# Joining the attention and the second FFN in one block, and beginning the FFN within the attention's last two slots

## The reference, cut to what matters

```
x = x + 0.5 * ffn(layernorm(x))      # first FFN
x = x + attention(layernorm(x))      # causal, 16 heads of 32, rotary, tanh soft cap
x = x + 0.5 * ffn(layernorm(x))      # second FFN, the same weights

def ffn(h):
    z = w_norm * h / rms(h)
    p = softmax(z @ w_router); top 4 of 32 experts for each token, in expert order, 128 slots an expert
    routed = sum over chosen experts of p * (silu(z @ w_gate) * (z @ w_up)) @ w_down
    shared = sigmoid(z @ w_sgate) * (silu(z @ sw_gate) * (z @ sw_up)) @ sw_down
    return h + routed + shared
```

## Time and profile before

| | |
|---|---|
| median of 3 runs | 1000.01 us |
| profiled execution | 997.65 us |
| its span, first to last instruction | 995.9 us |
| TensorE busy | 921.9 us, 93% |
| VectorE busy | 691.1 us, 69% |
| ScalarE busy | 534.3 us, 54% |
| GpSimd busy | 502.7 us, 50% |
| TensorE's mean granted clock | 0.983 |

### The profile page before, as it was taken

One profiled execution on the slowest core, in us unless ns is written; L12 is line 12 of the kernel. 1 busy time (PEld: TensorE's weight loads), 2 busy tenths in 40 slices (PEclk: granted clock), 3 DMA queues, 4 the chain that ended last, 5 costly groups with the idle time before them and its releaser, 6 DMA issues. The chain is left out here.

```text
span 995.9 us, 18354 instructions
## 1 busy us (share of the span) xinstructions
PE 921.9 (93%) x6274; PEld 690.3 (69%) x6274; DVE 691.1 (69%) x1702; ACT 534.3 (54%) x798; POOL 502.7 (50%) x534
## 2 busy tenths in 40 slices
PE   1999998999999899999999999839999989999997
PEld 1778885777778765666666666427888857777786
DVE  4888768644444769989989999646887676453435
ACT  3667652223233478878878878726666522232322
POOL 5342112565553467877878877623422124565630
PEclk9999999999999999999999999978999999999999
DMA  5432316677774510010010000112323156777735
GB/s 192 121 93 91 102 53 180 160 180 183 173 186 82 169 65 23 21 42 21 21 42 21 21 22 12 62 35 90 113 89 95 60 172 157 180 180 183 187 44 169
DMA packets 95434, 101.91 MB, mean 102 GB/s; under 512 B 18689, under 2 KB 86657, under 8 KB 95361
## 3 DMA queue, kind: packets, MB, share of 16 engines
q1 hardware_dynamic: 83072, 83.17, 27.3%
q0 software_dynamic: 12288, 17.83, 10.6%
HBM read 65.44 MB, written 35.54 MB: 101 GB/s over the span
## 5 line engine op out<-in xcount | busy, mean ns | idle before, releaser
L86 PE MATMUL gu<-x_hi,gu_hi 128*128 128x512 f32 x264 | 122.9, 465 | 4.0 <-DVE act_gu L1145 3.8
L691 POOL DMA_INDIRECT rows<-z_rows,slots x64 | 68.5, 1071 | 76.0 <-DVE slots L1136 57.3
L977 ACT CAST a_hi<-act_gu 128x512 fp32r<-128x512 f32 x96 | 59.2, 616 | 86.9 <-DVE act_gu L1145 74.5
L1570 ACT ACTIVATE capped_at<-scores_at 128x2048 f32<-128x2048 f32 x64 | 93.3, 1457 | 23.3 <-PE scores_at L1470 23.0
L87 PE MATMUL gu<-x_hi,gu_lo 128*128 128x512 f32 x264 | 105.6, 400 | 0.0
L88 PE MATMUL gu<-x_lo,gu_hi 128*128 128x512 f32 x264 | 105.6, 400 | 0.0
L1578 ACT ACTIVATE probs_at<-capped_at 128x2048 f32<-128x2048 f32 x64 | 95.2, 1487 | 2.5
L1639 POOL TENSOR_SCALAR_AFFINE_SELECT probs_at<-probs_at 128x1024 f32<-128x1024 f32 x64 | 86.6, 1357 | 18.4 <-ACT probs_at L1578 17.7
L86 PE MATMUL down<-down_hi,a_hi 128*128 128x256 f32 x300 | 94.2, 314 | 0.2 <-DVE a_lo L1155 0.2
L267 POOL TENSOR_TENSOR rstd_f<-var_in_f,neg_half 128x8 f32<-128x8 f32 x16 | 26.7, 1668 | 126.0 <-DVE var_in_f L262 126.0
L1025 ACT ACTIVATE y<-gu,rows 128x256 f32<-128x256 f32 x64 | 30.3, 473 | 109.9 <-PE gu L906 106.0
(11 more groups left out here) (245 smaller groups left out, 2605.5 us busy)
## 6 DMA issues: line engine op xcount, KB each, us to landing
w_gu<-in_w_gate SPq DMA_DIRECT2D x64, 176.0 KB, 2.6
w_gu<-in_w_up SPq DMA_DIRECT2D x64, 176.0 KB, 3.2
w_down<-in_w_down SPq DMA_DIRECT2D x64, 176.0 KB
z_rows<-z SPq DMA_DIRECT2D x16, 512.0 KB, 3.1
acc<-base SPq DMA_DIRECT2D x10, 512.0 KB, 3.4
out<-base SPq DMA_DIRECT2D x10, 512.0 KB, 3.4
x_f<-in_X SPq DMA_DIRECT2D x8, 512.0 KB, 4.6
xn_at<-acc SPq DMA_DIRECT2D x16, 256.0 KB, 2.7
```

The source lines that it names most:

```text
L86: nc.tensor.matmul(out, w_hi, x_hi, start=first, stop=False)
L691: pool.indirect_dma_start(out=gathered_rows[:, n, :], out_offset=None, in_=m.z_rows, in_offset=bass.IndirectOffsetOnAxis(ap=slots[:, e:e + ...
L1570: nc.scalar.activation(capped[:, u % 2, :, 0:n], scores[:, :, 0:n], ACT.Tanh, scale=QK_SCALE / SOFTCAP).then_inc(capped_ready, 1)
```

## The change

All three stages stand in one block, so the meeting of engines, the clearing of semaphores and the second meeting between attention and second FFN are gone; all semaphores are cleared once, at the end. Both FFNs use the same semaphores: `sem` hands out the existing one and notes what value the first FFN left it at, and every wait adds that value (`reached`). Some small tiles are placed earlier in memory so that what the FFN writes first doesn't lie on tiles the attention still uses.

The second FFN's first block is interleaved with the end of the attention:

- SyncE issues the loads of blocks 0 and 1 in slot 12 instead of slot 14.
- VectorE: `statistics` of block 0 opens slot 14, that of block 1 opens slot 15; the low parts of block 0 follow `divide(14, 1)` in slot 15.
- GpSimd: `scales` of block 0 stands ahead of slot 14's first `causal`, that of block 1 ahead of slot 15's first `causal`.
- ScalarE: two of the four `z` rows of block 0 after the second exponential of slot 14, two at that slot's end; the high parts in slot 15, ahead of its third cap.
- TensorE: `turn(0)` in slot 15, behind `weighted_values(14, 3)` and three waits; `output(14)` also waits for the low parts.
- The tail of sequence 15 is mixed into a new first slot of the second FFN, `slot_behind`, on all compute engines.

In the first FFN, the splitting of the attention's weights (11 pairs, L202 and L207) starts at piece 98 instead of 102.

The core of the diff (the shared semaphores' many lines are cut to a few; in all of the FFN's functions `wait_ge` becomes `reached`):

```diff
+        def sem(name, total=0):
+            if name not in m.shared:
+                m.shared[name] = (nc.alloc_semaphore(name=name), total)
+                ...
+            else:
+                begun[m.shared[name][0]] = m.shared[name][1]
+            return m.shared[name][0]
+
+        def reached(engine, signal, value):
+            engine.wait_ge(signal, begun.get(signal, 0) + value)
...
-        SPLITS_FROM = 3 * PIECES
+        SPLITS_FROM = LEAD + 5 * E // 2
...
@@ ffn, on_sync
             store_z(0)
             load_x(2)
             store_z(1)
+            if before:
+                before.wait_stored(sp)
...
@@ ffn, on_gpsimd
+            if before:
+                before.last_output(pool)
             make_base(0)
             for r in range(1, NB - 2):
-                front.scales(pool, r, r % 2)
+                if r > 1 or not before:
+                    front.scales(pool, r, r % 2)
                 make_base(r)
...
@@ ffn, on_tensor
+            def slot_behind(f, r, s):
+                before.scores_taken(pe)
+                chunk(0, 0)
+                before.residual_added(pe, SEQS - 1)
+                router(0)
+                before.tensor_last_values(pe)
+                turn_logits(f)
+                chunk(0, 1)
+                chunk(0, 2)
+                before.tensor_last_output(pe)
+                chunk(0, 3)
+                before.residual_added(pe, SEQS)
+                turn(r)
+                count(f)
+                chunk(0, 4)
+                router(r)
+                chunk(0, 5)
+                turn_logits(r)
+                for c in range(6, GU):
+                    chunk(0, c)
+                ...
...
@@ ffn, on_scalar
+            def slot_behind(f, r, s):
+                make_z(1)
+                before.probabilities_made(act)
+                silu_of(0, 0)
+                take_logits(0)
+                before.scalar_last_values(act)
+                silu_of(0, 1)
+                x_hi_parts(r)
+                exponentials(f)
+                a_hi_part(0, 0)
+                take_logits(r)
+                ...
...
@@ ffn, on_vector
+            def slot_behind(f, r, s):
+                before.vector_last_values(dve)
+                product(0, 0)
+                before.vector_last_low_part(dve)
+                top_experts(f)
+                before.vector_last_residual(dve)
+                x_lo_parts(r)
+                product(0, 1)
+                take_counts(f)
+                statistics(s)
+                before.sequences_stored(dve)
+                weigh(f)
+                a_lo_part(0, 0)
+                a_lo_part(0, 1)
+                product(0, 2)
+                top_experts(r)
+                ...
...
@@ attention, tensor_slot
             if behind:
                 weighted_values(b - 1, 1 - q, 3)
+            if following:
+                pe.wait_ge(v_copied, SEQS)
+                pe.wait_ge(turned_ready, SEQS * PIECES)
+                pe.wait_ge(x2_ready, SEQS - 2)
+                following.turn(0)
...
             score_unit(b, q, 3)
+            if following:
+                following.input_split(pe)
             if behind:
                 output(b - 1)
...
@@ attention, scalar_slot
             if further:
                 normalise(b + 2, held)
+            elif following and ahead:
+                following.make_z(0, range(0, 2))
+            elif following:
+                act.wait_ge(roped_ready, (SEQS - 1) * PIECES + 2)
+                following.x_hi_parts(0)
             cap(b, 2)
...
             if ahead:
                 copy_v(b + 1, 1 - q)
+                if following:
+                    following.make_z(0, range(2, TJ))
...
@@ attention, gpsimd_slot
             if further:
                 root(b + 2)
+            elif following:
+                following.front.scales(pool, b - (SEQS - 2), b - (SEQS - 2))
             causal(b, 0)
...
@@ attention, vector_slot
             if further:
                 statistics(b + 2)
+            elif following:
+                following.front.statistics(dve, b - (SEQS - 2), b - (SEQS - 2), 0)
...
+            if following and not ahead:
+                dve.wait_ge(roped_ready, (SEQS - 1) * PIECES + 2)
+                following.x_lo_parts(0)
...
+        def wait_stored(sp):
+            for n in range(HELD):
+                sp.wait_ge(stored[n], 16 * len(range(n, SEQS, HELD)))
+            sp.sem_inc(all_stored, 1)
...
+        def last_output(pool):
+            pool.wait_ge(out_ready, SEQS)
...
+        def tensor_last_values(pe):
+            weighted_values(SEQS - 1, 1, 3)
+            denominators(SEQS - 1, 1)
...
+        def scalar_last_values(act):
+            take_values(SEQS - 1, 1)
+            y_hi_part(SEQS - 1, 0)
+            y_hi_part(SEQS - 1, 1)
+
+        def vector_last_values(dve):
+            y_lo_part(SEQS - 1, 0)
+            invert(SEQS - 1, 1)
+            divide(SEQS - 1, 1)
...
@@ attention, on_sync
-                if b == SEQS - 2:
+                if b == SEQS - 4:
...
@@ build
-            run(ffn_before, middle)
-            run(ffn(nc, m, "2", m.acc2, front, ins))
-            nc.clear_and_free_semaphores(fronts.signals)
+            last = ffn(nc, m, "2", m.acc2, front, ins)
+            run(ffn_before, middle, last)
+            for stage in (fronts, ffn_before, middle, last):
+                nc.clear_and_free_semaphores(stage.signals)
             nc.all_engine_barrier()
```

More of the change, by code:

```diff
@@ L509, in ffn @@
[L509 to L520, removed]
+        z_ready = sem("z_ready", TJ * NB)
@@ new lines, in router, with make_z @@
+        def router(r):
+            reached(pe, lo_ready, KC * (r + 1))
+            h = held(r)
+            for k in range(KC):
+                last = split_matmul(nc, zT[0][:], m.router_hi[:, k, :], m.router_lo[:, k, :], x_hi[h][:, k, :],
+                                    x_lo[h][:, k, :], k == 0, k == KC - 1)
+            last.then_inc(lT_ready, 1)
+        def make_z(r, pieces=range(TJ)):
+            q = r % 2
+            reached(act, front.scales_ready, r + 1)
+            at_least(act, zT_ready, KC * (r - 1))
+            at_least(act, z_stored[q], 16 * (r // 2))
+            for j in pieces:
+                nc.scalar.activation(z[:, q, j, :], x[:, q, j, :], ACT.Identity, bias=front.z_shift[:, q, j:j + 1],
+                                     scale=front.z_scale[:, q, j:j + 1]).then_inc(z_ready, 1)
@@ L843, in slot @@
                     router(s)
+            def slot_behind(f, r, s):
[18 more added lines that the diff above has]
+                    chunk(0, c)
+                count(r)
+                turn(s)
+                for j in range(TJ):
+                    down_proj(0, j, range(MT))
+                router(s)
             def piece(p):
@@ L907, in down_expert @@
                 last.then_inc(y_ready, 1)
-            turn(0)
-            router(0)
-            for b in range(MERGED):
+            if before:
+                slot_behind(*ROUTES[0])
+            else:
+                turn(0)
+                router(0)
+                slot(0, *ROUTES[0])
+            for b in range(1, MERGED):
                 slot(b, *ROUTES[b])
@@ L1269, in copy_products @@
             def copy_products(e):
-                dve.wait_ge(prodT_ready, e + 1)
+                reached(dve, prodT_ready, e + 1)
                 at_least(dve, y_ready, e - 1)
                 dve.tensor_copy(prodT[:, e % 2], prodT_ps).then_inc(prodT_copied, 1)
-            statistics(1)
-            x_lo_parts(0)
-            if weights:
-                weights.low_gate_up(dve)
-            for b in range(MERGED):
+            if before:
+                slot_behind(*ROUTES[0])
+            else:
+                statistics(1)
+                x_lo_parts(0)
+                if weights:
+                    weights.low_gate_up(dve)
+                slot(0, *ROUTES[0])
+            for b in range(1, MERGED):
                 slot(b, *ROUTES[b])
@@ L1519, in output, with tensor_slot @@
             last.then_inc(out_ready, 1)
[L1521 removed]
+        def tensor_slot(b, q, behind=True, ahead=True, further=True, following=None):
             score_unit(b, q, 0)
@@ L1813, in on_tensor, with on_scalar @@
             tensor_slot(SEQS - 2, 0, further=False)
-            tensor_slot(SEQS - 1, 1, ahead=False, further=False)
-            weighted_values(SEQS - 1, 1, 3)
-            denominators(SEQS - 1, 1)
-            output(SEQS - 1)
-        def on_scalar(act, following=None):
+            tensor_slot(SEQS - 1, 1, ahead=False, further=False, following=following)
+        def on_scalar(act, before, following):
             scalar_slot(0, 0, 2, behind=False)
@@ L1845, in on_gpsimd, with on_vector @@
             gpsimd_slot(SEQS - 3, 1)
-            gpsimd_slot(SEQS - 2, 0, further=False)
-            gpsimd_slot(SEQS - 1, 1, ahead=False, further=False)
-            front.scales(pool, 0, 0)
-        def on_vector(dve, following=None):
```

(3 more changed lines are left out.)

448 lines of the change are left out of this document (247 added, 201 removed).

## The result

The changed kernel takes 990.7 us (median of 7 runs, 988.74 to 994.77) against 998.06 us of the kernel before beside it (995.9 to 1000.85): ratio 0.9926, 95% interval 0.9904 to 0.9949. Measured once more, beside the last experiments (e9), it is 989.87 us, 0.9903 [0.9882, 0.9924]. The forecast was 988.5 us, with 979.0 to 995.0 as its range, and faster.

The account below looks back on a forecast made before the run. TensorE bounds the kernel almost everywhere except the seam between attention and second FFN. Terms +3.1 + 4.3 + 1.0 - 0.5 - 19.6 - 0.7 = -12.4, plus 0.9, give -11.5: 1000.0 to 988.5 us, range 979.0 to 995.0.

Parts of the forecast that it names:

- slow restart: Down projection of block 0: TensorE restarts at a lower clock after idling between chunks 7 and 8, +0.9 us (0 to 3).
- The chain and its end: Seam: one chain followed up to weigh(0), set there by VectorE alone; what is gained there is gained at the end.
- Change 5: First FFN: earlier splits shorten TensorE's 1.48 us wait for block 7's product, -0.7 us (bounds 0 and -1.5).
- Change 3: Tail of sequence 15, last exponential to end of output(15): 13.3 us instead of 13.8, -0.5 us.
- Change 4: End of output(15) to weigh(0): 10.0 us instead of 29.6, set by block 2's load, -19.6 us.
- Change 1: Slots 14 and 15: GpSimd's scales ahead of the masks delay TensorE's weighted values, +3.1 and +4.3 us.
- Change 2: Slot 15: after TensorE's longer wait the score unit also runs at half clock, +1.0 us.
- The rival that the masks aren't delayed: Slots 14 and 15: exponentials pace the masks, so the 8.4 us loss is absent, 980.1 us; chance 20%.
- The rival of a persisting half clock: Half clock lasts from slot 15 into block 0, +6.1 us, 994.6 us; chance 15%.

Follow-up runs that it names:

- e9: The changed kernel as it is, timed again beside e10 and e11: 989.87 us, 0.9903 of the kernel before.
- e1: The changed kernel without the interleaving in slots 14 and 15, with the joining and earlier splits kept: 990.27 us, 0.9921 of the kernel before.
- e5: The changed kernel plus 16 and 36 unused filler matmuls in TensorE's waits for the masks of slots 14 and 15: 988.69 us, 0.9926 of the kernel before.
- e10: The kernel of e5 timed again, beside e9: 988.01 us, 0.988 of the kernel before.
- e7: e3 with statistics(0) between VectorE's two turns of sequence 15 and rotary work ahead of slot 14's scales on GpSimd: 979.66 us, 0.983 of the kernel before.
- e2: The changed kernel with GpSimd's scales of block 1 behind slot 15's second mask instead of ahead of its first: 985.13 us, 0.9865 of the kernel before.
- e3: e2 with slot 14's scales behind its first mask too, and all four z products at slot 14's end: 984.55 us, 0.9872 of the kernel before.
- e4: The changed kernel with VectorE's statistics of block 2 behind block 0's third product instead of ahead of weigh(0): 991.76 us, 0.9938 of the kernel before.
- e11: The kernel of e3 timed again, code unchanged: 985.14 us, 0.9849 of the kernel before.
- e6: The kernel before with only the first FFN's earlier splits: 997.11 us, 1.0004 of the kernel before.
- e8: e7 with statistics, z and turning of block 2 moved later in the second FFN's block 0: 980.34 us, 0.9833 of the kernel before.

## Why the prediction was right, point by point

The direction, the chain and the gain were right; the closeness of the number is in part luck. The change of the median is -7.4 us and that of the profiled executions -8.9, where -11.5 was forecast. The losses were forecast too small by 5.0 us (2.7 for masks and clock, 2.3 for the tail); 2.2 of these are hidden by the first FFN's part and by the slow restart that didn't come, which have other causes. And the forecast starts from a median of 1000.0 us, while the kernel before took 998.06 beside the changed one: that alone brings 988.5 nearer to 990.7 by 2 us.

**The chain and its end** held. From `weigh(0)` to the end of the kernel it is 307.4 us before and 307.3 after, so the sum up to `weigh(0)` is the result. Between slot 14's first scores and `weigh(0)` it is, in the prediction's own terms:

| term | forecast | measured |
|---|---|---|
| up to slot 14 (Change 5) | -0.7 | -2.0 |
| slot 14's first scores to the last exponential (Changes 1 and 2) | +8.4 | +11.1 |
| last exponential to the end of `output(15)` (Change 3) | 13.3 - 13.8 = -0.5 | 15.6 - 13.8 = +1.8 |
| end of `output(15)` to `weigh(0)` (Change 4) | 10.0 - 29.6 = -19.6 | 10.0 - 29.6 = -19.6 |
| slow restart in block 0 | +0.9 | 0 |
| sum | -11.5 | -8.7 (span: -8.9) |

The measured ones are differences of the rows above: (654.17 - 610.28) - (645.06 - 612.31), then 669.75 - 654.17 (GpSimd's base starts as `output(15)` ends), then 679.73 - 669.75.

**Change 4**, the gain, came as worked out: the load decides, and VectorE waits 2.45 us for it. e1 divides the 19.6 us. It joins the stages and changes no slot, and gets 8.2 of them (29.6 to 21.4 us): that is the meeting. The other 11.4 are first steps of the second FFN that stand ahead of `output(15)` now, and the interleaving pays for them with the 11.1 and 1.8 us of the table.

**Change 1** has the right mechanism and nearly the right size. With the clock filled up, e5 and e10 reach the last exponential 40.7 us after slot 14's first scores, against 32.75 before: +8.0, where 7.4 was forecast. In e7, with the masks ahead, it is 34.6. The 0.6 between them is no more than what GpSimd's rows add: in each of the two scales one small instruction took some 0.7 instead of 0.2 us. e2 and e3 show the cause: with the scales behind the masks, the waits shrink. The rival that the masks aren't delayed (20%) is out. Slot 14's weighted values came 3.6 us later (3.1 forecast), slot 15's 10.2 (7.4), and the latter includes the clock.

**Change 2**, the clock, is the step that was mis-sized: 1.0 us forecast, and 11.1 - 8.0 = 3.1 measured, or 2.8 by e9 and e10 (43.6 - 40.7). I took half clock for slot 15's score unit alone. It stood in slot 14 as well, behind a wait of 2.28 us, and in slot 15 it lasted through the score units and the first ten matmuls of `output(14)` (0.41 instead of 0.28 us each). The row for this was at hand: the earlier trace rows has 1.94 us behind a wait of 2.31, and slot 14's new wait was forecast at about that length. It was only asked of slot 15. How long it lasts isn't fixed: in e9, the same kernel, it ends within slot 15's score unit (1.72 us), and `output(14)` runs at full clock. The rival of a persisting half clock (15%) is right in kind, not in place: block 0 ran at full clock. The Trainium skill, "TensorE: Matmul & The Clock Gate", Part 1, says that half rate is the default and that activity releases it. The trace agrees: a clock of 0.57 follows the wait of 5.39 us, and in e5, with fillers in the waits, the same groups take 1.06 and 1.14 us.

**Change 3** failed in size: 15.6 us instead of 13.3. The sum let ScalarE's table load follow `z` at once. It waited 2.13 us for `chunk(0, 0)`, which stands behind `output(14)` on TensorE. In e5, e7, e9 and e10 that wait is 0.56 to 0.58 us, and the stretch from the exponential to the residual's start is 14.6 instead of 16.1 us. So 1.5 us of the excess of 2.3 are the half clock once more, in the slow `output(14)` of that execution (and of e4's: 2.13 and 16.1 as well); most of the rest is the 0.6 us wait that the sum left out.

**Change 5** came out above its bounds in the profiled execution (2.0 us, with 1.5 as the bound), but its cause gives less: the wait shrank by 1.2 us, and e11 against e3 shows 6.7 us of scatter in this part with the code unchanged. e6 finds no gain in time from the splits alone. The term should have been given as unproved.

**The slow restart** of 0.9 us didn't come: from 669.50 the clock is 1.00. TensorE waits 2.18 us for a product there, and the matmul behind it took 0.50 us, as the first of `chunk(0, 0)` did at full clock (657.58).

## What to carry to other kernels

When two stages are joined, try the plain join first: the meeting itself may be most of the gain. Here the plain join gives 0.8%, and interleaving the next stage's first steps adds nothing until they are put behind, not ahead of, the instructions that the old stage waits for; then it is 1.3% to 1.7%. Price a queue's new guests by every instruction, on the queue that they enter, and price a new wait of TensorE twice: the wait, and the half speed that may follow it.

## What was not expected of the hardware

- The same wait is not always followed by half clock: 2.28 us in slot 14 was in all profiled executions that had it (1.93 or 1.94, and 2.09 us, behind it), 1.87 and 1.88 us in slot 14 of e3 and e11 was not. A wait of 1.60 us in an early slot was in e11 (1.49 and 2.09 us behind it), and the same wait of 1.60 us in e3, with the same code, was not (1.06 and 1.14). So a wait's length alone didn't decide it in these rows.
- Small GpSimd instructions on 4 elements per partition took some 0.2 us, and now and then one took about 0.7. That isn't wholly random: in slot 14 it is the instruction of line 273 in all eight profiled executions in which the scales stand ahead of slot 14's first rotary product (e3 and e11 among them), and in e7 and e8, where they stand behind it, none. What causes it was not looked into.
- At the end of the first FFN a late adding DMA holds a load, the load holds VectorE's statistics, and these hold the product behind them. In e11 against e3 this is 5.1 of the 6.7 us by which two executions of one kernel differ. Putting the product ahead of those statistics on VectorE could take the scatter away; it wasn't tried.
- Issuing block 2's load ahead of `output(15)` wasn't tried either: it takes the buffer from which the base of block 0 is made, and GpSimd makes that base only once `output(15)` is done.
